# A graph network on one core: the rows that enter at chunks 1 to 3 split into two f32r halves and multiplied with adjacency and identity in one product

## What is computed

```python
# first network, on nodes 0 to 24 of each graph: five groups of nodes, two graph convolutions each
for g, idx_list in enumerate(GROUPS):
    adj_g = adj[:, idx][:, :, idx]
    h = _graph_conv(x[:, idx, :], adj_g, W1[g], b1[g])
    out_g = _graph_conv(h, adj_g, W2[g], b2[g])
    fused = fused.at[:, idx, :].add(norm_w[g] * out_g)
x = layernorm(x + fused)
# second network: five steps of a gated unit
A = (adj != 0)
h = x
for l in range(5):
    m = h @ weight[l]
    agg = einsum('bij,bid->bjd', A, m)
    h = gru_cell(agg, h, w_ih, w_hh, b_ih, b_hh)
out = layernorm(x + h * mask)
```

## Time and profile before

| what | value |
|---|---|
| median of 3 runs | 537.79 us (537.71 to 539.58) |
| the profiled execution's own time | 539.44 us |
| its span | 537.2 us |
| mean granted clock of TensorE over the span | 0.985 |
| PE busy | 516.6 us, 96% |
| DVE busy | 435.4 us, 81% |
| ACT busy | 368.5 us, 69% |
| POOL busy | 250.9 us, 47% |

### The profile page before, as it was taken

How to read it: one execution, slowest core, us unless ns; L and a number is a source line. 1 busy time by engine, 2 the same in 40 slices (tenths; PEclk the granted TensorE clock), 3 DMA queues, 4 the chain that set the end, 5 groups by cost and what they waited for, 6 DMA issues and landing times.

```text
span 537.2 us, 8518 instructions
## 1 busy us (share of the span) xinstructions
PE 516.6 (96%) x2991; PEld 442.1 (82%) x2991; DVE 435.4 (81%) x965; ACT 368.5 (69%) x681; POOL 250.9 (47%) x301
## 2 busy tenths in 40 slices
PE   7999999999999999999999999999999999999970
PEld 5888889888888889888888888888888888888850
DVE  4489765899979877889989986688988989778785
ACT  2448665767866676787785666687776678777644
POOL 6658513458532354457633243445552254423235
PEclk8999999999999999999999999999999999999995
DMA  5767610000000000000000000000000001000002
GB/s 143 185 181 201 162 33 5 1 1 0 2 1 0 6 27 21 21 20 21 1 1 1 1 0 22 21 20 21 0 2 1 1 1 35 25 21 0 1 0 79
DMA packets 35563, 17.29 MB, mean 32 GB/s; under 512 B 4305, under 2 KB 35482, under 8 KB 35522
## 3 DMA queue, kind: packets, MB, share of 16 engines
q1 hardware_dynamic: 32489, 15.12, 10.7%
q10 hardware_dynamic: 2393, 1.41, 1.0%
q0 software_dynamic: 640, 0.22, 0.3%
HBM read 12.54 MB, written 4.19 MB: 31 GB/s over the span
## 4 chain that ended last, share of the span: by engine, by line
PE 89%; DVE 4%; ACT 2%; POOL 1%; DMA 1%; issue 1%; ACTq 1%; POOLq 0%; DVEq 0%
PE p L1206 20%; PE p L1208 20%; PE p L1207 19%; PE p L1200 13%; PE p L1193 8%; PE p L1086 3%; PE p L1060 2%; PE p L1079 1%; PE p L1069 1%; PE p L1004 1%; DMA zg<-in_L_gnn_weight_dram 1%; PE p L1124 1%; DVE st L885 1%; DVE cg L969 1%; POOL rs L432 1%
## 5 line engine op out<-in xcount | busy, mean ns | idle before, releaser
L470 POOL TENSOR_TENSOR dg<-hT,ng 128x512 f32<-128x512 f32 x80 | 126.4, 1579 | 257.8 <-ACT ng L677 257.8
L1206 PE MATMUL p<-ghi,wf 128*128 128x512 f32 x240 | 101.1, 421 | 0.0
L1206 PE MATMUL p<-hhi,wh 128*128 128x512 f32 x237 | 99.7, 421 | 0.0
L1208 PE MATMUL p<-ghi,wf 128*128 128x512 f32 x240 | 94.4, 394 | 0.0
L1207 PE MATMUL p<-glo,wf 128*128 128x512 f32 x240 | 93.6, 390 | 0.0
L1208 PE MATMUL p<-hhi,wh 128*128 128x512 f32 x237 | 93.2, 393 | 0.0
L1207 PE MATMUL p<-hlo,wh 128*128 128x512 f32 x237 | 92.5, 390 | 0.0
L969 DVE SCALAR_TENSOR_TENSOR cg<-p,biasc,rg 128x512 f32<-128x512 f32 x80 | 59.8, 748 | 38.2 <-ACT rg L659 37.2
L659 ACT ACTIVATE rg<-p,gb 128x512 f32<-128x512 f32 x80 | 55.4, 692 | 34.4 <-PE p L1208 28.6
L677 ACT ACTIVATE ng<-cg,biasc 128x512 f32<-128x512 f32 x80 | 57.9, 723 | 22.9 <-DVE cg L972 22.6
L1200 PEld LDWEIGHTS p<-an,nat 128*128 128x128 f32 x512 | 66.9, 191 | 5.1
(11 more groups left out here) (147 smaller groups left out, 852.4 us busy)
## 6 DMA issues: line engine op xcount, KB each, us to landing
xn<-in_x_dram SPq DMA_DIRECT2D x8, 512.0 KB, 4.7
an<-in_adj_dram SPq DMA_DIRECT2D x8, 512.0 KB, 7.5
out_dram<-xn SPq DMA_DIRECT2D x16, 256.0 KB, 2.3
xt<-in_x_dram SPq DMA_DIRECT2D x16, 50.0 KB
w<-in_L_gnn_W_dram ACTq DMA_DIRECT2D x1, 640.0 KB, 4.8
w<-in_L_gnn_W_dram SPq DMA_DIRECT2D x1, 640.0 KB, 5.4
zg<-in_L_gnn_weight_dram ACTq DMA_DIRECT2D x1, 320.0 KB, 4.1
xt<-in_x_dram SPq DMA_DIRECT2D x8, 36.0 KB
```

What stands on the lines that cost most here:

```text
L470: nc.gpsimd.tensor_tensor(dg[:, w.k % 2, :], hT[:, w.slot, :], ng[:, w.k % 2, :], ALU.subtract).then_inc(d_ok, 1)
L1206: MM(bank[:], w[:, 0, cols], xhi, start=start, stop=False)
L1208: return MM(bank[:], w[:, 1, cols], xhi, start=False, stop=stop)
```

## The change

The rows of a visit that enters at chunks 1 to 3 are no longer transposed. They are split by nodes' rows into a high and a low f32r half (`er`), and each half is the stationary operand of one f32r matmul per graph whose moving operand has 256 columns: the graph's adjacency (128 columns) and an identity (128 columns, kept as row `B` of `an`, which is now f32r). The output has sums and state side by side; for four graphs it fills the two banks PG and PL, which are now one tensor `PGL` with the views `SUMS` and `STATE`. So four transposes and four f32 matmuls (eight records) become eight f32r matmuls at the end of window k.

- ACT makes the high half of the rows for the third and fourth visit of a chunk (in windows 19 and 20 of the chunk before), DVE for the first and second (both at the end of window 17). POOL makes all low halves, `low_rows`, ahead of `dg` in windows 18 to 21.
- ACT copies `hhi` and `hT` of the entering visit at the head of window k+1, ahead of sigmoid r (before: in window k, ahead of sigmoid z).
- DVE makes `glo` at the end of window k only after that `hT` copy (a new wait), and `hlo` in window k+1 ahead of L969, out of PSUM (before: at the end of window k out of SBUF).
- PE's combined product waits for `hlo` of the visit that entered one window before, and so does the ordinary `aggregate` of window 22, 42 and 62.
- PE's `adjacency(c)` is at the end of window 2 of each chunk for all c; ACT and DVE scale at the head of window 3.
- Adjacency is loaded to `raw` (16 graphs), and the ones go from `raw` to `an`; the load of chunk c waits until the ones of chunk c-1 are made. `nat`, `ghi` and `glo` have fewer buffers.

```diff
 def made(k):
-    return SLOTS + 1 if k == SLOTS - 1 else SLOTS if k == SLOTS else k + 1
+    return k + 2 if k % PER == SLOTS - 1 else k if k % PER == SLOTS else k + 1
...
+def coming_in(k):
+    return ALL_WINDOWS[k].enter if 2 <= k < WINDOWS else None
...
-        an = sb("an", [128, B, N])
+        an = sb("an", [128, B + 1, N], f32r)
+        raw = sb("raw", [128, CB, N])
-        nat = sb("nat", [128, SLOTS, SB, D])
-        ghi = sb("ghi", [128, SLOTS, COLS], f32r)
-        glo = sb("glo", [128, SLOTS, COLS], f32r)
+        nat = sb("nat", [128, SB, D])
+        er = sb("er", [128, 2, 2, SB, D], f32r)
+        ghi = sb("ghi", [128, 2, COLS], f32r)
+        glo = sb("glo", [128, 2, COLS], f32r)
...
+        PGL = ctx.enter_context(nc.psum_tensor("pgl", [128, 2 * 512], f32))
+        P += [PGL[:, 0:512], PGL[:, 512:1024]]
+        both = PGL[:].rearrange("p (q o n) -> p q o n", q=SB, o=2)
+        SUMS, STATE = both[:, :, 0, :], both[:, :, 1, :]
...   SP
+            load_chunk(sp, 1)
+            sp.wait_ge(a0_ok, 2)
+            sp.wait_ge(a_ok, 2)
+            load_graphs(sp, 1)
...   (c = 2, 3, after the stores of visits 0 to 3 for c = 3)
+                sp.wait_ge(a_ok, SLOTS * c - 2)
+                load_graphs(sp, c)
...   POOL
+            nc.gpsimd.tensor_copy(an[:, B, :], ident[:])
...
-                nc.gpsimd.tensor_scalar(ab, ab, 0.0, 0.0, ALU.is_equal, ALU.is_equal).then_inc(a_ok, 1)
+                nc.gpsimd.tensor_scalar(ab, raw[:, visit % SLOTS * SB:(visit % SLOTS + 1) * SB, :], 0.0, 0.0, ALU.is_equal, ALU.is_equal).then_inc(a_ok, 1)
...
+            def low_rows(k):
+                visit = ALL_WINDOWS[k].enter
+                half = 2 * (visit // SLOTS - 1) + visit % 2 + 1
+                pool.wait_ge(ehi_ok if visit % SLOTS < 2 else ehi_act, half)
+                pool.wait_ge(G_ps, k + 1)
+                nc.gpsimd.tensor_tensor(er[:, visit % 2, 1], xn[:, visit * SB:(visit + 1) * SB, :], er[:, visit % 2, 0],
+                                        ALU.subtract).then_inc(elo_ok, 1)
...   (window loop, ahead of dg)
+                if coming_in(w.k) is not None:
+                    low_rows(w.k)
...   ACT (window loop, ahead of nat and sigmoid r)
+                if coming_in(k - 1) is not None:
+                    high_state(coming_in(k - 1), None)
+                    state(coming_in(k - 1), None)
+                    if coming_in(k - 1) % SLOTS < 2:
+                        high_rows(coming_in(k - 1) + 2)
...   (after sigmoid r)
-                if w.enter is not None and k >= 2:
-                    state(w.enter, PL)
-                    high_state(w.enter, PL)
...   DVE
             def lo_neighbours(m, bank):
                 dve.wait_ge(ghi_ok, m + 1)
+                if coming_in(m - 2) is not None:
+                    dve.wait_ge(hT_ok, coming_in(m - 2) + 1)
...
+            def lo_entering(m):
+                dve.wait_ge(hi_ok, made(m))
+                TT(by_graph(hlo[:, m % SLOTS, :]), STATE, by_graph(hhi[:, m % SLOTS, :]), ALU.subtract).then_inc(lo_ok, 1)
...   (window loop, just ahead of the wait for r_ok and L969)
+                if coming_in(k - 1) is not None:
+                    lo_entering(k + 1)
...   (end of the window)
-                if k >= 2 and w.enter is not None:
-                    lo_state(k + 2)
                 if k >= 2 and w.feed:
                     lo_neighbours(k + 2, PG)
+                if c is not None and w.i == Plan.ROWS:
+                    high_rows(c * SLOTS)
+                    high_rows(c * SLOTS + 1)
...   PE
+            def enter_and_aggregate(k):
+                visit = ALL_WINDOWS[k].enter
+                for q in range(SB):
+                    b = visit * SB + q
+                    moving = an[:, b:B + 1:B - b, :]
+                    MM(both[:, q], er[:, visit % 2, 0, q, :], moving, start=True, stop=False)
+                    last = MM(both[:, q], er[:, visit % 2, 1, q, :], moving, start=False, stop=True)
+                last.then_inc(G_ps, 1)
...
-                    if w.i == Plan.ADJ and c > 1:
-                        pe.wait_ge(hi_ok, k + 2)
-                        pe.wait_ge(hT_ok, SLOTS * c)
-                        pe.wait_ge(x_ok, 2 * PACK * (c - 1))
-                        adjacency(c)
...
-                if w.enter is not None and k >= 2:
-                    pe.wait_ge(ob_ok, (NG - 1) * (w.enter // SLOTS + 1))
-                    pe.wait_ge(hi_ok, k + 2)
-                    pe.wait_ge(hT_ok, w.enter)
-                    enter(w.enter, PL)
...
                 if w.feed and k >= 2:
                     pe.wait_ge(glo_ok, 3 if k == 2 else k + 2)
+                    if coming_in(k - 1) is not None:
+                        pe.wait_ge(lo_ok, made(k + 1))
                     if w.enter is not None:
                         pe.wait_ge(a_ok, w.enter - 1)
-                        aggregate(k + 2, PG, entering(w.enter))
+                        pe.wait_ge(elo_ok, w.enter - SLOTS + 1)
+                        pe.wait_ge(ob_ok, (NG - 1) * (w.enter // SLOTS + 1))
+                        pe.wait_ge(hT_ok, w.enter)
+                        enter_and_aggregate(k)
...
-                if k == adjacency_in(1) - 1:
-                    pe.wait_ge(hT_ok, SLOTS)
-                    adjacency(1)
+                if c is not None and w.i == Plan.Y - 1:
+                    pe.wait_ge(hT_ok, SLOTS * c)
+                    pe.wait_ge(lo_ok, made(k + 1))
+                    if c > 1:
+                        pe.wait_ge(x_ok, 2 * PACK * (c - 1))
+                    adjacency(c)
```

More of the change, by code:

```diff
@@ L94, in made, with first_window @@
 def made(k):
-    return SLOTS + 1 if k == SLOTS - 1 else SLOTS if k == SLOTS else k + 1
-def adjacency_in(c):
-    return Plan.Y if c == 1 else Plan.ADJ
+    return k + 2 if k % PER == SLOTS - 1 else k if k % PER == SLOTS else k + 1
+def first_window(visit):
+    return visit // SLOTS * PER + visit % SLOTS
+def coming_in(k):
+    return ALL_WINDOWS[k].enter if 2 <= k < WINDOWS else None
 def next_chunk(w):
@@ L610, in high_state @@
             def high_state(visit, bank):
-                act.wait_ge(X_ps, visit + 1)
-                nc.scalar.copy(hhi[:, visit % SLOTS, :], bank[:]).then_inc(hi_ok, 1)
+                if visit < SLOTS:
+                    act.wait_ge(X_ps, visit + 1)
+                    nc.scalar.copy(hhi[:, visit % SLOTS, :], bank[:]).then_inc(hi_ok, 1)
+                else:
+                    act.wait_ge(G_ps, first_window(visit) + 1)
+                    nc.scalar.copy(by_graph(hhi[:, visit % SLOTS, :]), STATE).then_inc(hi_ok, 1)
             def state(visit, bank):
@@ L616, in state, with high_rows @@
                     act.wait_ge(lo_ok, made(visit))
+                    nc.scalar.copy(hT[:, visit % SLOTS, :], bank[:]).then_inc(hT_ok, 1)
                 else:
-                    act.wait_ge(X_ps, visit + 1)
-                nc.scalar.copy(hT[:, visit % SLOTS, :], bank[:]).then_inc(hT_ok, 1)
+                    nc.scalar.copy(by_graph(hT[:, visit % SLOTS, :]), STATE).then_inc(hT_ok, 1)
+            def high_rows(visit):
+                act.wait_ge(ln1_ok, visit + 1)
+                nc.scalar.copy(er[:, visit % 2, 0], xn[:, visit * SB:(visit + 1) * SB, :]).then_inc(ehi_act, 1)
             def aggregated(m, bank):
                 act.wait_ge(G_ps, m + 1)
-                nc.scalar.copy(ghi[:, m % SLOTS, :], bank[:]).then_inc(ghi_ok, 1)
+                if coming_in(m - 2) is None:
+                    nc.scalar.copy(ghi[:, m % 2, :], bank[:]).then_inc(ghi_ok, 1)
+                else:
+                    nc.scalar.copy(by_graph(ghi[:, m % 2, :]), SUMS).then_inc(ghi_ok, 1)
             norm1(0, HALVES[0])
@@ L861, in lo_neighbours, with high_rows @@
                 dve.wait_ge(ghi_ok, m + 1)
-                TT(glo[:, m % SLOTS, :], bank[:], ghi[:, m % SLOTS, :], ALU.subtract).then_inc(glo_ok, 1)
+                if coming_in(m - 2) is not None:
+                    dve.wait_ge(hT_ok, coming_in(m - 2) + 1)
+                if coming_in(m - 2) is None:
+                    TT(glo[:, m % 2, :], bank[:], ghi[:, m % 2, :], ALU.subtract).then_inc(glo_ok, 1)
+                else:
+                    TT(by_graph(glo[:, m % 2, :]), SUMS, by_graph(ghi[:, m % 2, :]), ALU.subtract).then_inc(glo_ok, 1)
+            def lo_entering(m):
+                dve.wait_ge(hi_ok, made(m))
+                TT(by_graph(hlo[:, m % SLOTS, :]), STATE, by_graph(hhi[:, m % SLOTS, :]), ALU.subtract).then_inc(lo_ok, 1)
+            def high_rows(visit):
+                dve.wait_ge(ln1_ok, visit + 1)
+                dve.wait_ge(G_ps, first_window(visit) - 2)
+                nc.vector.tensor_copy(er[:, visit % 2, 0], xn[:, visit * SB:(visit + 1) * SB, :]).then_inc(ehi_ok, 1)
             def end_step(k, s):
@@ L1199, in aggregate @@
                 for q in range(SB):
-                    last = MM(bank[:, q * N:(q + 1) * N], src(q), an[:, b + q, :], start=True, stop=True)
```

(4 more changed lines are left out.)

50 lines of the change are left out of this document (27 added, 23 removed).

## The result

| | before | after |
|---|---|---|
| median of 6 runs each | 538.73 us (537.71 to 539.98) | 543.04 us (541.85 to 544.87) |
| profiled execution, its span | 539.44, 537.2 | 541.85, 540.0 |

A forecast was written before the change was run, and what follows sets the result against it. TensorE bounds the kernel now, with VectorE nearly so; after the change a 5.96 us ring replaces it. Losses of 1.4 + 1.4 + 0.6 = +3.4 us give 541.2 us against the 537.79 median (542.8 as profiled), range 539.7 to 544.2.

The forecast's parts named there:

- the two places of the loss: Window 23's start, 0.6 us late after the entering windows, and `neighbours` in window 23, 1.4 late with the 0.6 contained.
- rival (a): Entering windows: TensorE stays the bound, the combined product pays in full, 3.0 us come back, 534.8; chance 0.15.
- The wide product: TensorE, end of entering windows: eight f32r matmuls of 256 columns take 1.0 us, between 0.12 and 0.24 each.
- Rival (c): TensorE's combined product: each wide matmul costs 0.24 like 512 columns, 1.92 for eight; +9, 547 us; chance 0.10.
- The ring: Entering windows: VectorE and ScalarE waits close from one L969 to the next, 5.96 us against TensorE's 5.68.
- Window 22: Longer turn of 6.2 us through the stepped high half; window 23 starts at 181.35 against 180.77, 0.6 late.
- `na`: ScalarE's adjacency scaling, head of window 23: ready 4.65 us after L969, making `neighbours` 1.4 late, an earlier 0.6 contained.
- Rival (b): Window 23: `na` is ready when `neighbours` is due, only 3 x 0.6 = 1.8 us remain, 539.6; chance 0.20.
- Entry: End of window 17: two VectorE row copies, 0.40 each after `dg`, put window 18's L969 at 155.63 instead of 155.13.
- the rule: VectorE two-SBUF-input instructions or fast copies and GpSimd SBUF reads block each other; row copies wait 0.26 us per chunk.
- The sum: Whole kernel: chunks 1 and 2 pay 1.4 us each at their ends, chunk 3 pays 0.6, together +3.4.

The follow-up runs named there:

- experiment 7: Changed kernel with `na` ahead of the stepped high half, ring cut, first row copy a window earlier, `hT` ahead of sigmoid r except window 22: 537.98 us against 538.94, 0.9975.
- experiment 3: Changed kernel with ScalarE's `hT` and rows' high half after sigmoid r, and the visit's `hlo` right behind `glo`: 537.71 us in one run.
- experiment 4: Changed kernel with one more VectorE sum, about 0.6 us, ahead of `glo` of each entering visit, 12 in all: 552.71 us in one run.
- Experiment 1: Changed kernel with ScalarE's `na` ahead of the stepped state's high half instead of behind it: 540.78 us in one run.
- experiment 8: Changed kernel with `na` ahead of the stepped high half, first row copy a window earlier, ring cut with `hT` after sigmoid r: 537.03 us against 539.14, ratio 0.9959.
- experiment 5: Changed kernel with the 12 additional VectorE sums ahead of `glo` in four ordinary windows of chunks 1 to 3 instead: 547.67 us in one run.
- experiment 2: Kernel before with only the adjacency of chunks 2 and 3 moved to where the changed kernel has it: 541.98 us against 539.07, ratio 1.0069.

## Why the prediction was right, and where its numbers were off

The time, its sign and the two places of the loss came as forecast: 542.8 for an execution like the profiled one, 541.2 for the median, +3.4 in all; measured +3.8 by the ratio, and a median of 543.04, inside the forecast's bounds of 539.7 to 544.2. (Of the 1.8 between 541.2 and 543.04, 0.9 is the kernel before, whose median is 538.73 over six runs and was 537.79 over three. The prediction gives the upper bound once as 544.2 and once as 544.6, and rival (a) as 534.8 and 535.2; nothing hangs on the 0.4.) Point by point:

- **The wide product.** 1.0 us taken, 0.94 (experiment 7, where TensorE comes to it without a pause) to 1.03 measured. Rival (c), 0.24 each, falls. What the combined product is worth came to 0.3 us in a window (experiment 7). The Trainium skill (TensorE: Matmul & The Clock Gate, Back-to-back issue gap) gives 262 cycles for 256 columns in its table of isolated gaps. At 2.4 GHz that makes an estimate of 0.109 us; the trace has 0.118.
- **The ring.** Its links and their order are those of the trace, and cutting it takes the loss away (experiment 3), while adding to it is paid in full (experiment 4). Its length was 6.08 and not 5.96: nearly all of the 0.12 is one link, `hT`'s start to `glo`'s, 0.70 where I had put 0.57 + 0.03. The copy lasted 0.60, and VectorE started 0.10 after its end: I had taken the release of tanh by VectorE, 0.03, for a release the other way.
- **Window 22.** L1039 to L1039 was 6.40 (171.72 to 178.12), 6.2 forecast; from there to the start of window 23 1.83, where 1.65 was forecast. With three turns of the ring 0.12 longer, and an entry 0.2 earlier (below), this makes 1.1 late at the start of window 23 for the 0.6 that I gave.
- **`na`.** From L1039 of window 22 to `neighbours` 4.60, forecast 4.65; window 23 pays 0.70 for it, forecast 0.8. Experiment 1 gives it back whole. Rival (b), that it is hidden, falls: window 23 would have stayed at 7.46, and it is 8.16.
- **Entry.** The forecast had the first row copy start only when `dg` ends, 0.26 late, and 0.40 for each copy. VectorE's and GpSimd's timelines:

```profile
151.66 0.53 DVE L931 CAST er<-xn 128x512 fp32r<-128x512 f32 x1
152.12 0.41 DVE L931 CAST er<-xn 128x512 fp32r<-128x512 f32 x1
```

```profile
150.63 1.29 POOL L510 TENSOR_TENSOR dg<-hT,ng 128x512 f32<-128x512 f32 x1 [2.18 <-ACT ng L730]
```

  The copy's start is recorded while `dg` still runs, but it lasts 0.53, where the second, which starts while GpSimd is still, lasts 0.41, and to the next start it takes 0.45 for 0.34. Its end hangs on `dg`: in all 33 cases of the eight kernels with these copies in which one starts beside `dg`, it ends 0.28 us after `dg` does. So the wait is there, and costs 0.12 and not 0.26, since part of the copy passes beside `dg`. That bears out the rule from the Trainium skill (SBUF — State Buffer, Who interferes with whom) that the forecast used, with a smaller price. L1039 of window 18 came 4.51 after the window's start instead of 4.71. The other half of the rule was seen too: `hlo` out of PSUM took 0.68 where it had taken 1.78 out of SBUF beside `dg`. GpSimd's first `low_rows` ended at 152.28 + 1.42 = 153.70 and the combined product of window 18 started at 153.90, 0.25 later than with the usual step, as forecast.
- **Rival (a)**, that the product pays in full, failed at the place it named, the first window whose product waits for `hlo`: that is window 19 already (`hlo` ends at 159.64 in after, the product starts at 159.74, and the window is 5.84 long where experiment 7 has 5.54). Rearranged (experiment 8), the change does win, 0.9 us in the loop where the rival had 3.0.
- **The sum.** The loop lost 4.54, not 3.4: 1.8, 1.8 and 0.95 for my 1.4, 1.4 and 0.6. I had forecast nothing for the time around the span, which fell by 0.45. The two errors have opposite signs, so it is in part luck that the total came out within half a us: the loop was forecast 1.1 too low.

## What to carry to other kernels

A new wait is cheap or dear by what stands behind it in its engine's program: follow the instructions behind it until they come back to the thing waited for, add the links from start to start, and compare that one number with the bound engine's window. When a saving of 0.25 us a window turns into a loss with no engine busy, look for such a ring, and break it at the link whose result is needed last: here the state copy that only TensorE's next product wants. Two orders that each repair one window can differ in the next, so measure the loop window by window, and before calling an engine's time slack in a window, read that engine's row for that window. An addition can also cost where it does not stand: in experiments 4 and 5 two instructions that start 0.056 us apart instead of 0.059 went with two windows half a us longer in all.

## What the runs showed of the hardware

- An f32r matmul of 256 columns whose moving operand lies in two pieces (an adjacency and the identity, 1 to 48 blocks of 128 columns apart) steps at 0.118 us, half of the 0.23 to 0.24 of 512 columns, although each has a new stationary operand. The first of eight takes 0.20 when TensorE stood still ahead of it.
- A VectorE copy of 128x512 from SBUF to SBUF, f32 to f32r, takes 0.41 us and 0.34 to the next start when it starts while GpSimd is still. When it starts beside GpSimd's `dg` it ends 0.28 after that (33 of 33 cases; 0.53 to 0.57 long). The other way about, `low_rows` lasts 1.42 when it starts beside such a copy (152.28 in after) and 1.28 to 1.30 in the windows without one.
- The stretch ahead of window 1 goes with TensorE's granted clock there. Stretches of before, then of after, 8 to 16 us:

```profile
8.00:12.00 4.00, 3.55 (x12) 2.19 (x13) 1.50 (x6) 1.23 (x3) 2.50 (x3) 0.70 0.70 173
12.00:16.00 4.00, 4.00 (x26) 2.98 (x25) 2.76 (x9) 1.44 (x3) 2.42 (x8) 0.87 0.93 270
```

```profile
8.00:12.00 4.00, 3.61 (x16) 2.24 (x17) 2.36 (x9) 1.71 (x4) 2.79 (x4) 1.00 0.74 196
12.00:16.00 4.00, 3.56 (x33) 3.20 (x31) 3.08 (x12) 1.91 (x6) 2.97 (x8) 1.00 0.87 240
```

  Window 1 starts at 43.36 and 41.41 in these. Of the difference of 1.95, 1.60 lies in eight matmuls of 384 columns (L1004, L1075 in after), which take from 9.77 to 14.03 in before and from 9.60 to 12.26 in after. Of the ten profiles three have a granted clock of 1.00 (2.4 GHz) in both stretches (window 1 starts at 41.35 to 41.59), three 0.57 and then 1.00 (42.38 to 42.47), and four 0.69 to 0.75 and then 0.82 to 0.88 (43.16 to 43.36). Why the clock fell in some executions and not in others no run shows. The kind does not go with the change: experiments 7 and 8 were of the last, as before was. So 2 us of difference between two single profiles of this kernel mean nothing until the granted clock of its first 16 us is compared.
- A kernel with the change takes 1.83 to 1.87 us beside its span, one without 2.32 to 2.38 (means over 5 to 17 runs; experiment 2 is among the latter). Which part of the change does it wasn't tried.
